# Transfers of a graph network kernel on one Trainium2 core: another outer dimension, another split and another order

## The reference

```python
attn = ex / denom[dst]
agg = segment_sum(attn[:, :, None] * v[src], dst).reshape(n, HC)
x_attn = agg + x @ Wskip + bskip
h = x_attn @ Wlin + blin + x_attn[:, :OUT_DIM]
```

## Time and profile before

| | |
|---|---|
| runs shown | median 2340.5 us of 3 (2332.41 to 2343.21) |
| profiled execution | 2341.79 us, its span 2340.0 us |
| mean granted clock of TensorE | 0.883 |
| busy: PE, DVE, ACT, POOL | 1781.9, 1303.4, 920.2, 622.8 us |
| moved by DMA | 265.14 MB, mean 113 GB/s |

### The profile page before, as it was taken

The page is one execution under the profiler, slowest core; times in us unless marked ns, Lnnn a source line. Parts: engine busy times, 40 slices in busy tenths (PEclk is TensorE's granted clock), DMA queues, the critical chain, the costliest instruction groups (busy, mean ns, idle before and its releaser), DMA issues. The chain is left out here.

```text
span 2340.0 us, 31896 instructions
## 1 busy us (share of the span) xinstructions
PE 1781.9 (76%) x10958; PEld 1518.8 (65%) x10958; DVE 1303.4 (56%) x2945; ACT 920.2 (39%) x1702; POOL 622.8 (27%) x526
## 2 busy tenths in 40 slices
PE   7997995999999567766894000059998999999686
PEld 5765994777777456555793000058887888888576
DVE  5352454899989325556452000035556888788766
ACT  4331344888888211113120000033244655556421
POOL 0001005666787000010010000001122545544234
PEclk9998997999999878887997555579999999999889
DMA  6832767888887232212311111120150112120442
GB/s 213 256 125 99 247 195 184 209 213 210 210 209 202 101 108 94 96 60 95 93 55 54 55 54 73 70 78 20 64 170 19 36 28 49 30 52 9 158 139 100
DMA packets 176232, 265.14 MB, mean 113 GB/s; under 512 B 54562, under 2 KB 101153, under 8 KB 174579
## 3 DMA queue, kind: packets, MB, share of 16 engines
q1 hardware_dynamic: 121723, 192.10, 26.2%
q0 software_dynamic: 49760, 62.92, 10.5%
q10 hardware_dynamic: 4616, 8.40, 1.0%
HBM read 198.55 MB, written 85.86 MB: 122 GB/s over the span
## 5 line engine op out<-in xcount | busy, mean ns | idle before, releaser
L1053 POOL DMA_INDIRECT edge_rows<-xn_store,edge_index x200 | 280.5, 1403 | 243.3 <-issue 181.6
L135 PE MATMUL psum<-xt_hi,fc_hi 128*128 128x250 f32 x320 | 95.0, 297 | 312.4 <-DVE hid_lo L2060 309.1
L135 PEld LDWEIGHTS psum<-xt_hi,fc_hi 128*128 128x128 f32 x320 | 62.1, 194 | 315.3 <-DVE hid_lo L2060 311.3
L2526 POOL TENSOR_TENSOR mprob<-mprob,mrden 125x1250 f32<-125x1250 f32 x80 | 181.5, 2271 | 216.4 <-DVE mrden L2632 216.0
L2033 DVE TENSOR_TENSOR w_lo<-w_raw,w_hi 128x512 fp32r<-128x512 f32 x16 | 10.7, 684 | 302.9 <-ACT w_hi L1821 302.5
L2555 ACT ACTIVATE mprob<-psum,mbias 125x1250 f32<-125x1250 f32 x80 | 104.3, 1304 | 153.0 <-DVE mbias L2641 153.0
L1268 DVE TENSOR_TENSOR edge_xt_lo<-psum,edge_xt_hi 128x500 fp32r<-128x500 f32 x200 | 130.4, 675 | 52.2 <-ACT edge_xt_hi L1140 52.2
L2639 DVE TENSOR_REDUCE mmin<-psum 125x1 f32<-125x512 f32 (+1 forms) x240 | 126.8, 584 | 46.5 <-PE psum L2798 46.2
L1428 PE MATMUL psum<-ident,edge_rows 125*128 125x125 f32 x800 | 120.6, 274 | 23.1 <-POOLq L1060 23.1
L1767 POOL TENSOR_TENSOR x_res<-x_res,xs_chunk 125x1024 f32<-125x1024 f32 x5 | 12.3, 2453 | 466.5 <-DVE xs_chunk L2007 466.5
L2816 PE MATMUL psum<-ident,mprob 125*125 125x125 f32 x800 | 117.8, 292 | 17.9 <-DVE ptm_lo L2646 9.8
(11 more groups left out here) (519 smaller groups left out, 5626.5 us busy)
## 6 DMA issues: line engine op xcount, KB each, us to landing
slots_in<-blank_rows SPq DMA_DIRECT2D x40, 513.0 KB
t_store<-t_part SPq DMA_DIRECT2D x20, 1000.0 KB, 4.9
t_row<-t_store SPq DMA_DIRECT2D x50, 400.0 KB, 7.2
y_store<-y_rows SPq DMA_DIRECT2D x50, 200.0 KB
y_tile<-y_store SPq DMA_DIRECT2D x50, 200.0 KB
q_chunk<-q_store SPq DMA_DIRECT2D x40, 250.0 KB, 5.4
edge_attr<-in_attr SPq DMA_DIRECT2D x50, 125.0 KB
moe_xg<-slots_in SPq DMA_DIRECT2D x17, 256.5 KB, 3.6
```

The source lines that it names most:

```text
L135: nc.tensor.matmul(out, lh, rh, start=start, stop=False)
L1053: nc.gpsimd.indirect_dma_start(xe[t % RING][:, s, :], None, g.xn_store, bass.IndirectOffsetOnAxis(ap=index[t % RING][:, s, 0:1], axis=0)). ...
L2526: nc.gpsimd.tensor_tensor(prob[:, n % 4, :], prob[:, n % 4, :], rden[:, n % 4:n % 4 + 1].broadcast_to([P, N]), ALU.mult).then_inc(p_ready, 1)
```

## The change

- Blank rows: `slots_in` is seen as 128 rows by n blocks, so that the outer dimension of both sides is 128 and not n; a transfer fills 4 blocks instead of 2, and there are 20 + 1 transfers instead of 40 + 1.
- Inside a window the 100 pairs are ordered node by node (4 heads each) instead of head by head. `y_store` becomes 1250 rows of 2048 values, and a value tile is 125 full rows, read with two transfers, of 112 and 13 rows, instead of five.
- Transfers of 125 rows of `skip_out`, attributes, `acc` (both ways), `xin` and `last_xin` are split in the same way (`in_two`), with their semaphores counted to 32.
- The constants are moved after the ten skip stores.
- `y_load(0)` is issued two windows sooner, ahead of `y_store(t - 1)`. Behind the score loop the wait for `xe_low` is gone, and the attributes and the second value tile are asked for between the edge lists.

```diff
+    ROWS = slice(0, 112), slice(112, P)
+    def in_two(eng, dst, src_, arrived):
+        for rows in ROWS:
+            eng.dma_start(dst[rows], src_[rows]).then_inc(arrived, 16)
...
-            for h in range(HEADS):
-                for pos in range(PER_TILE):
-                    sp.dma_start(consts[WIN * h:WIN * h + WIN, NT * pos:NT * pos + NT],
-                                 g.cd[WIN * pos:WIN * pos + WIN, NT * h:NT * h + NT]).then_inc(fin_in, 16)
             sp.dma_start(v_raw[0][:], g.vl_store[0]).then_inc(v_first, 16)
...
             for t in range(NT):
                 sp.wait_ge(skip_added, t + 1)
-                sp.dma_start(g.base_store[t * P:(t + 1) * P, :], skip_out[:, t % 4, :]).then_inc(skip_stored[t % 4], 16)
+                in_two(sp, tiles(g.base_store)[:, t, :], skip_out[:, t % 4, :], skip_stored[t % 4])
+            for h in range(HEADS):
+                for pos in range(PER_TILE):
+                    sp.dma_start(consts[h:HW:HEADS, NT * pos:NT * pos + NT],
+                                 g.cd[WIN * pos:WIN * pos + WIN, NT * h:NT * h + NT]).then_inc(fin_in, 16)
...
-                sp.dma_start(g.y_store[t], y[t % 2][:]).then_inc(y_stored[t % 2], 16)
+                sp.dma_start(g.y_store[WIN * t:WIN * (t + 1), :].rearrange("n (h d) -> (n h) d", h=HEADS), y[t % 2][:]).then_inc(y_stored[t % 2], 16)
...
-                for pos in range(PER_TILE):
-                    sp.dma_start(y_in[r % 2][WIN * pos:WIN * pos + WIN, :, :],
-                                 g.y_store[PER_TILE * r + pos].rearrange("(h n) d -> n h d", h=HEADS)).then_inc(y_back[r % 2], 16)
+                for rows in ROWS:
+                    sp.dma_start(y_in[r % 2][rows, :], tiles(g.y_store)[rows, r, :]).then_inc(y_back[r % 2], 16)
...
-                sp.dma_start(attr[t % 2][:], w["attr"][bass.ds(first, RANGE), :].rearrange("(p s) c -> p s c", s=SLOTS_E)
-                             ).then_inc(attr_in[t % 2], 16)
+                in_two(sp, attr[t % 2][:], w["attr"][bass.ds(first, RANGE), :].rearrange("(p s) c -> p s c", s=SLOTS_E), attr_in[t % 2])
...
+                    if t == WINDOWS - 3:
+                        sp.wait_ge(y_done, WINDOWS - RING + 1)
+                        y_load(0)
                     if t:
                         y_store(t - 1)
-                    if t == WINDOWS - 1:
-                        sp.wait_ge(y_done, WINDOWS - RING + 1)
-                        y_load(0)
                 sp.wait_ge(s_done, KT * WINDOWS)
                 sp.wait_ge(other_ready, WINDOWS)
                 sp.wait_ge(xe_ready, WINDOWS)
-                sp.wait_ge(xe_low, 2 * WINDOWS)
-                firsts = [edges_in(t) for t in range(RING)]
-                attr_load(0, firsts[0]), attr_load(1, firsts[1])
-                y_load(1)
+                firsts = []
+                for t in range(RING):
+                    firsts.append(edges_in(t))
+                    if t < 2:
+                        attr_load(t, firsts[t])
+                    if t == 1:
+                        y_load(1)
                 y_store(WINDOWS - 1)
...
-                    sp.dma_start(g.acc[:, 2 * c:2 * c + 2, :], pair(g.base_store, c)).then_inc(base_in, 16)
+                    in_two(sp, g.acc[:, 2 * c:2 * c + 2, :], pair(g.base_store, c), base_in)
...
-            link(nc.gpsimd.iota(ids[:], pattern=[[0, HEADS], [1, WIN]], base=0, channel_multiplier=0, allow_small_or_imprecise_dtypes=True))
+            link(nc.gpsimd.iota(ids[:], pattern=[[1, WIN], [0, HEADS]], base=0, channel_multiplier=0, allow_small_or_imprecise_dtypes=True))
...
-                nc.scalar.activation(t_hl[t % 2][:].rearrange("p q (h n) -> p q h n", h=HEADS),
+                nc.scalar.activation(t_hl[t % 2][:].rearrange("p q (n h) -> p q h n", h=HEADS),
                                      t_row[t % 3][:].rearrange("p h q n -> p q h n"), ACT.Copy).then_inc(t_made, 1)
...
+                names = ids[0:P, 0:HW:HEADS]
...
-BLANKS = NE * SLOTS // 256
+BLANKS = NE * SLOTS // 512
...
-                dst = g.slots_in[128 * first:128 * (first + n), :].rearrange("(i p) d -> i p d", p=128)
-                src = g.blank.rearrange("(i p) d -> i p d", i=1).broadcast_to([n, 128, D + 1])
+                dst = g.slots_in[128 * first:128 * (first + n), :].rearrange("(i p) d -> p i d", p=128)
+                src = g.blank.rearrange("p (i d) -> p i d", i=1).broadcast_to([128, n, D + 1])
...
-                blanks(2 * i, 2)
-            blanks(2 * BLANKS, 1)
+                blanks(4 * i, 4)
+            blanks(4 * BLANKS, 1)
...
-        g.y_store = nc.dram_tensor("y_store", [WINDOWS, HW, D], F32, kind="Internal").ap()
+        g.y_store = nc.dram_tensor("y_store", [N, HEADS * D], F32, kind="Internal").ap()
```

More of the change, by code:

```diff
@@ L793, in graph_attention @@
     index = [at(f"edge_index{i}", [P, SLOTS_E, 2], I32, 9 + i / 32) for i in range(RING)]
-    y_in = [at(f"y_tile{i}", [P, HEADS, D], F32, kb) for i, kb in enumerate((12, 84))]
+    y_in = [at(f"y_tile{i}", [P, HEADS * D], F32, kb) for i, kb in enumerate((12, 84))]
     yt_hi = [at(f"yt_hi{i}", [128, HEADS, KT, P], F32R, kb) for i, kb in enumerate((20, 36))]
@@ L888, in skip_over @@
         for i in range(4):
-            eng.wait_ge(skip_stored[i], 16 * len(range(i, NT, 4)))
+            eng.wait_ge(skip_stored[i], 32 * len(range(i, NT, 4)))
     def parts_over(eng):
@@ L1013, in _ @@
                         sp.wait_ge(o_added, 2 * c)
-                        sp.dma_start(pair(g.base_store, c - 1), g.acc[:, 2 * c - 2:2 * c, :]).then_inc(base_out, 16)
+                        in_two(sp, pair(g.base_store, c - 1), g.acc[:, 2 * c - 2:2 * c, :], base_out)
                     if step == 5 and c < FIN:
@@ L1017, in _ @@
                             sp.wait_ge(xin_used, 2 * c)
-                        sp.dma_start(fin.xin[:], pair(w["x"], c)).then_inc(xin_in, 16)
+                        in_two(sp, fin.xin[:], pair(w["x"], c), xin_in)
                 sp.wait_ge(o_added, NT)
-                sp.dma_start(pair(g.base_store, FIN), g.acc[:, 2 * FIN:, :]).then_inc(base_out, 16)
+                in_two(sp, pair(g.base_store, FIN), g.acc[:, 2 * FIN:, :], base_out)
                 sp.wait_ge(params, turn + 1)
                 sp.wait_ge(pass_done, 4 * turn + 4)
-                sp.wait_ge(base_out, 16 * NC)
+                sp.wait_ge(base_out, 32 * NC)
                 sp.sem_inc(pass_over, 1)
@@ L1091, in _ @@
                     if step == 9 and c < FIN:
-                        pool.wait_ge(xin_in, 16 * c + 48)
+                        pool.wait_ge(xin_in, 32 * c + 16 + 64)
                         nc.gpsimd.tensor_tensor(fin.xin[:], fin.xin[:], bc(fin.beta[:], 2), ALU.add).then_inc(xin_ready, 1)
@@ L1185, in attr_hi @@
             def attr_hi(t):
-                act.wait_ge(attr_in[t % 2], 16 * (t // 2) + 16)
+                act.wait_ge(attr_in[t % 2], 32 * (t // 2) + 32)
                 if t >= 2:
@@ L1247, in _ @@
                 if t >= 4:
-                    dve.wait_ge(skip_stored[t % 4], 16 * (t // 4))
+                    dve.wait_ge(skip_stored[t % 4], 32 * (t // 4))
                 nc.vector.tensor_tensor(skip_out[:, t % 4, :], skip_bank(t), row1[0:P, 0, :], ALU.add).then_inc(skip_added, 1)
@@ L1310, in hots @@
                 edges, shift = own_edges(t)
+                names = ids[0:P, 0:HW:HEADS]
                 nc.vector.scalar_tensor_tensor(hot[t % 2][:, :, window(t)], edges.unsqueeze(2).broadcast_to([P, SLOTS_E, WIN]), shift,
-                                               bc(ids[0:P, 0:WIN], SLOTS_E), ALU.add, ALU.is_equal).then_inc(hot_ready, 1)
+                                               bc(names, SLOTS_E), ALU.add, ALU.is_equal).then_inc(hot_ready, 1)
             def attr_lo(t):
@@ L1329, in add_out @@
             def add_out(r):
-                dve.wait_ge(base_in, 16 * NC)
+                dve.wait_ge(base_in, 32 * NC)
                 dve.wait_ge(o_done, r + 1)
@@ L1336, in finish @@
                 if step == 10:
-                    dve.wait_ge(base_out, 16 * c + 16)
+                    dve.wait_ge(base_out, 32 * c + 32)
                     dve.wait_ge(agg_out, 2 * c + 2)
@@ L1464, in turn_values @@
                 if h == 0:
-                    pe.wait_ge(y_back[r % 2], 16 * PER_TILE * (r // 2 + 1))
+                    pe.wait_ge(y_back[r % 2], 32 * (r // 2 + 1))
                 if n >= 2:
@@ L1468, in turn_values @@
                 for k in range(KT):
-                    last = nc.tensor.transpose(yt_bank(n)[:, k, :], y_in[r % 2][:, h, k * 128:(k + 1) * 128], g.ident[0:P, 0:P])
+                    last = nc.tensor.transpose(yt_bank(n)[:, k, :], y_in[r % 2][:, h * D + k * 128:h * D + (k + 1) * 128], g.ident[0:P, 0:P])
                 last.then_inc(yt_done, 1)
```

2 lines of the change are left out of this document (1 added, 1 removed).

## The result

| | before | after |
|---|---|---|
| median of 4 runs each, us | 2339.52 | 2050.34 (2047.79 to 2053.14) |
| ratio to before | | 0.877, 95% interval 0.874 to 0.879 |
| span of the profiled execution, us | 2340.0 | 2046.0 |
| mean granted clock | 0.883 | 0.946 |

The change saves 289 us. The forecast was 382, and its range ended at 2020; the result lies 30 us above it. Against the same spans (294 us) the missing 88 us sit in three places, and each shows in one view.

The account below looks back on a forecast made before the run. It took blank writes on two engines, holding SyncE's queue and delaying `w_raw`, as the main stall. Terms 295 + 12 + 14 + 55 + 4 + 2 = 382, from 2341.8, gave 1960 us; range 1925 to 2020.

Parts of the forecast that it names:

- blanks: Blank writes to `slots_in`: on 16 engines at 27.5 GB/s each, PE's whole 294.3 us wait for `hid_lo` goes; gain 295.
- score loop (copy with a step): Score loop: the stepped copy to `t_hl` adds at most 0.9 us, inside ACT's 1.1 us slack per window; taken as 0.
- output loop: Output loop: value tiles on 16 engines bring attributes sooner; 4.3 us a turn, 159 us; gain 55, bounds 20 and 74.
- first value tile, attributes, `acc`: Between score and output loops: earlier `y_load(0)` gains 12; faster `acc` and earlier attributes gain 14, bounds 3 and 29.
- skip stage: Skip stage: constants behind the stores give back up to 13.5 us, 9 lost again; sum 4, bounds -4 and 13.
- `base_out`: End of the output loop: 500 KB on five engines takes 4 us, with the change 1.5; gain 2.
- One sign of being wrong: Blanks stage: `hid_lo` waited for over 30 us, listed beside blanks that still hold the queue and turns over 5 us.
- The lower bound, 266: Blanks term if each byte counts twice, 180 GB/s: blanks take 118 or 119 us, a stall of 28 or 29 remains.
- copies inside memory are slow: Rival: blanks at 120 GB/s take 177 us, 87 us of stall stay, total 2047; chance 0.08.
- the first rival: Output loop keeps its pace: two-buffer attribute chain, added transfers or DVE set the turn; 55 falls to about 5, 2010; chance 0.14.
- The first value tile as 12 of its own: End of score loop: `y_load(0)` issued near 752, landed when PE wants it; 11.65 us wait goes, taken as 12.
- the prediction's lowest terms: All terms at their lower bounds: 266 + 10 + 3 + 20 - 4 + 0 = 295, giving 2047.

Follow-up runs that it names:

- blanks_only: The kernel before with one part of the change, the blanks as 20 transfers of 128 rows by 4 places; 2071.2 us.
- head_major: Changed kernel with the old head-outer order inside a window and each store of y made of four transfers; 2020.9 us.
- blanks_wide: Changed kernel with the blanks in 20 transfers over 16 engines, as contiguous pieces of four rows, 8208 bytes; 2013.8 us.
- blanks_16: Changed kernel with the blanks in 5 transfers, 16 places outermost, each piece a whole place of 128 rows; 2014.7 us.
- y_one: Changed kernel with each value tile loaded in one transfer of 125 rows of 8 KB, not 112 and 13; 2073.0 us.
- ring4: Changed kernel with four buffers for edge attributes instead of two, the first four windows' attributes asked for between the edge lists; 2039.7 us.
- attr_one: Changed kernel with each window's attributes in one transfer of 125 rows, as before the change; 2048.8 us.
- y_late: Changed kernel with the first value tile loaded where it was before, at the last window; 2041.4 us.
- acc_spread: Changed kernel with only the first pair of `acc` loaded ahead of the output loop, other pairs and first expert's weights during it; 2034.7 us.
- consts_spread: Changed kernel with the score constants loaded a window at a time behind the parts of the second head; 2032.4 us.

## Why the prediction was wrong

Two steps failed, with about the same loss: each of 16 engines was taken to copy the blanks at the 27.5 GB/s that two had reached (35 us), and the slower copy to `t_hl` was taken to fit into ACT's idle time (33 us). A third, the pace of the output loop, was right in kind and mis-sized by 16 us. Right were the sign, what bound the kernel (blanks on two engines that held SyncE), the count of engines from the outer dimension, and the order of the gains. By term, from the spans:

| term | predicted | measured | |
|---|---|---|---|
| blanks | 295 | 260 | 35 short |
| score loop (copy with a step) | 0 | -33 | 33 short |
| output loop | 55 | 39 | 16 short |
| first value tile, attributes, `acc` | 26 | 22 | 4 short |
| skip stage | 4 | 3.4 | |
| `base_out` | 2 | 3.5 | |

The measured entries come from stretches of the two timelines, each before against after: the first load of `t_row` at 364.7 and 361.3; from there to the end of the score loop 410.2 and 443.6; to the end of the first long wait on attributes 56.7 and 34.9; to the last `base_store<-acc` 212.9 and 174.0; to the next stage's first load 13.9 and 10.4. The blanks have what is left of the 294 us, since nothing behind them was changed. Alone, in blanks_only, they gave 266; the difference is within the spread of the stretch behind the first blank. One sign of being wrong that the prediction named came up: `hid_lo` waited for over 30 us (34.3).

*The copy with a step, taken as 0.* It was bounded rightly at twice the time, 0.9 us (0.785 measured), and then set against ACT's idle time in a window, 1.1 us. That is a sum over the window. Idle time at one place does not cover work at another: the copy stands behind the probabilities and ahead of PE's scores. It cost 33.4 us over 50 windows, 0.67 each. head_major shows it.

*Blanks at 27.5 GB/s for each engine.* The rate was read at two engines and carried to 16, and the sentence "two engines lost nothing" weighed only the double traffic. With the outer dimension the packets went from 44 KB to 2 KB, and an engine's rate from 27 to 10.4 GB/s. The packets of the trace before would have told the first half of this. The rest of the reasoning holds: at the measured 166 GB/s the prediction's own count leaves 128 - 83 - 7 = 38 us of stall, and 35 were found; blanks_wide gives 36.5 back. Even with long packets 27.5 didn't carry over: 16 engines at 350 GB/s are 22 each. The lower bound, 266 (267 by its own rows, 295 - 28), was nearer, but for a wrong reason: it took 180 GB/s, half of the highest rate seen, for a copy that reads and writes. That halving is refuted: blanks_16 copied at 350 GB/s. The Trainium skill, "DMA: Bandwidth & Descriptors", section Specifications, has about 358 GB/s as the memory's limit for a core; by this trace it can't be a limit on the bytes read and written together. That it limits bytes counted once is not shown: from 1115 to 1125 us, with loads beside the first blanks, blanks_16 moved 418 GB/s. The rival "copies inside memory are slow" (chance 0.08) had the kind of effect right, at 120 GB/s with 87 us of stall where 166 and 35 were measured, and named no cause. That its 2047 lies 3 us from the result is luck: it leaves out the copy and takes the output loop at 55.

*The output loop at 4.3 us a turn.* Its mechanism was right: y_one takes it away whole. The size was off: 4.8 a turn, 38.2 us for eight where 34.4 were forecast. About 2 of the 3.8 us are PE's own work, put at 30 for eight turns and 32.4 in the profile (97.31 us busy in the 115 us from 871 to 986). The rest are waits for attributes, to which the chain of two buffers that the first rival named adds (ring4: 36 us for eight turns, 4.5 each). The rival's full form, only 5 us gained, did not come. The Trainium skill's fixed cost of a transfer, about 2 us (same page, section "Anatomy of one DMA — SWDGE (gpsimd) path", where it is measured on transfers that GpSimd issues; these are SyncE's), weighed in the prediction at 100 us for the split, did not show: attr_one has 50 transfers fewer and the same time.

*The first value tile as 12 of its own.* y_late gives back 7.45 and takes 6.1 from the next wait: by itself the early load is worth 1 to 2 us by the waits, and at most the 5 us by which the first blank comes later. The 22 us of this stretch were not taken apart further. acc_spread shows that `acc` and the weights in front of the attributes held half of the wait that was left (10.5 of 19.9).

*Constants in the skip stage.* Forecast 9 us lost again, found 10.4; this step was right to a microsecond, and consts_spread takes it away.

The result, 2050, lies even below what the prediction's lowest terms give together, 2047. The range could not hold it because the copy had no term below zero, and because the range rested on "they will not all fall on one side": blanks, loop, tile with `acc`, and copy all did.

## What to carry to other kernels

When the outer dimension of a transfer is changed to reach more engines, look also at how long the contiguous pieces become, and read the packets before and after: 16 engines with 2 KB packets moved 166 GB/s, 8 with 44 KB packets 218. Contiguous pieces of 8 KB were enough. Slack of an engine hides added work only if it lies between that work and whoever waits for it; read the order of the timeline, not the busy share. Of a stall that ends on a load, ask what stands ahead of that load in full queues: moving three megabytes that nobody needed yet took 10.5 us from the wait, though only half of it outlived the loop. And judge a small edit by the place in the timeline where its effect ends, not by the whole time alone, when another stretch spreads by 10 us.

## What was not expected of the hardware

- ACT's copy of 128 x 800 elements took 874 ns, and 1659 with a step of four elements on the written side; written without a step and read with one of 200 elements, 1630. PE's products with the result took as long as before (465 and 468 ns at L135). DVE's `edge_hot`, which reads the names with a step of four now, took 328 ns instead of 253; head_major, which takes that back too, has the output loop at the same pace.
- One engine, copying from memory to memory, moved a piece of 2052 bytes in 0.19 us (10.4 GB/s), pieces of 8208 bytes in 16 x 20 x 0.937 / 670 = 0.45 us (16 GB/s in the mean of the stretch), and packets of 44 KB at 27 GB/s when two or eight engines ran, 22 when 16 did. From on-chip memory a piece of 2052 bytes took 16 x 40 x 1.019 / 3905 = 0.17 us, hardly less.
- A copy in memory on 16 engines reached 350 GB/s over 10 us, close to the 360 of the fastest stretch shown before.
- With the same blank transfers, the stretch from the first blank's issue to the first `mprob` took 345 to 360 us in the profiles of eight kernels that changed nothing in it, and the rate of the blanks differed with it: 188 GB/s from 1120 to 1240 us in y_late, 170 in the changed kernel. What sets that was not found.
